# Softmax sums as four column tiles of 32, and a rounded copy moved from VectorE to ScalarE, in an attention and mixture-of-experts kernel

## The chip, the core and the metric

One core of a Trainium2 chip. The metric is the device time of one execution in microseconds, lower is better. The engines named below are TensorE (PE), VectorE (DVE), ScalarE (ACT), GpSimd (POOL) and SyncE (SP), which issues most of the transfers. PEld is TensorE's loading of weights.

## The reference

`x` and `ctx` are (4, 512, 512) in fp32: 4 batches of 512 rows (tokens) by 512. The first half is a cross-attention whose heads cut the row axis, so that 64 rows are one head and the 512 columns are positions; the softmax runs over 512 columns of `ctx`, after both sides are normalized over the 64 rows of a head:

```
qn, kn = l2norm over the head's 64 rows
qk = 5.0 * einsum('bhdq,bhdk->bhqk', qn, kn);  sm = softmax(qk)
x  = x + einsum('bhqk,bhdk->bhdq', sm, vh)        # q from layernorm(x), k = v = ctx
```

The second half is a mixture of 4 experts with top-2 routing and a capacity of 512 tokens each: router logits of 2048 tokens, a selection of the 512 best tokens per expert, then `gelu(tok @ W1[i]) @ W2[i] * p` with W1 512x2048 and W2 2048x512, added to the rows that were chosen.

## The kernel before, in words

The attention runs in 16 units of 128 rows, that is two heads each (`UNITS`, `unit(u, behind, ahead)`). Each engine has its own program for a unit, and the programs are written out by hand: what an engine does in unit n belongs partly to units n+1 to n+3 (statistics, normalized queries, keys) and partly to n-1 to n-3 (inverse sums, residual, router logits). `run_units` (lines 341 to 356) writes out units 0 to 3, runs units 4 to 11 as a loop of four rounds with two units in each, and writes out units 12 to 15. The arguments `behind` and `ahead` say how many units lie before and after, up to 4 and 3.

What the attention computes for a unit: TensorE transposes the normalized `x_norm` (`transpose_queries`, `bank_m`), ScalarE squares, VectorE sums (`sum_query_squares`), POOL takes the inverse root (`query_norms`), VectorE widens it (`widen_queries`, `wide_q`), TensorE transposes it back (`spread_queries`, `bank_m`), and VectorE multiplies: `queries(u, follow)` writes `q_f` (fp32), `q_hi` (rounded to fp32r) and `q_lo = q_f - q_hi`, with `normalize(follow)` of a later unit between them. Keys are split likewise into `k_hi` (ScalarE, `round_keys`) and `k_lo` (POOL). `scores(u, t)` on TensorE makes block t of four, 128 keys by 512 positions for both heads, out of three products. ScalarE's `exponentials(u, t)` takes them to `prob` (two instructions, one for each head). TensorE's `weighted_values` multiplies with the values, and `sums` adds the probabilities over the keys: VectorE has added the four blocks of `prob` in pairs (`half_sum[h][n]`, head h, half n), and `sums` multiplies them with a matrix of ones, 64 columns for each head, the two halves accumulated in PSUM (`o_ps[1]`).

ScalarE copies the result (`take_sums`, `p_sum`). Each row of a head's 64 is the same, so SyncE's `spread_inverse` takes one row per head, spreads it over 64 partitions as 8 numbers each (`few`, 128x8), VectorE inverts (`invert_few`), SyncE writes it to DRAM and reads it back broadcast (`p_inv`, 128x512), and `residual` multiplies one unit later. Only the last unit inverts the whole tile on VectorE (`invert_sums`).

The order of the work is set by each engine's own queue, which is strictly in order, and by semaphores. In the last third of a unit VectorE runs `residual`, `statistics_x2`, `widen_queries`, `take_logits` and `normalize_x2` of earlier and later units; `take_logits` (line 815) reads the router's result from `bank_t`, and TensorE's next unit begins with `values`, which writes `bank_t` (line 1246) and waits for it (line 1327). SyncE's order in the loop is, for each unit: load of a later x and ctx, `few`, `inv_dram`, `p_inv`, store of the sum and store of x2n (lines 443 to 451).

The experts follow: 16 chunks of `up` (line 1423) and `down` (lines 1450 to 1453) for each expert, with weights split into high and low parts.

Of the kernel before, what the change touches and what calls it, by code (L numbers as in the profile page):

```python
# [15 lines left out]
ALU = mybir.AluOpType  # L16
# [20 lines left out]
RAW_BUFS, SPLIT_BUFS = 2, 4  # L37
AHEAD = 2
FEW = 2 * D // P
DVE_HEADS, POOL_HEADS = (0, 1), ()  # L40
XT_AT = 10
FIND_AT = 8
# [51 lines left out]
def xattn_moe_kernel(nc, x, ctx_in, Wg, bg, W1, W2, consts, out):  # L94
# [6 lines left out]
    with ExitStack() as stack:  # L101
# [68 lines left out]
        with ExitStack() as phase:  # L170
# [16 lines left out]
            o_sb = [att(f"o_sb{n}", [P, D]) for n in range(2)]  # L187
            p_sum = att("p_sum", [P, D])
            half_sum = [[att(f"half_sum{h}{n}", [P, D]) for n in range(2)] for h in range(2)]
            few = att("few", [P, FEW])  # L190
            few_inv = att("few_inv", [P, FEW])
            p_inv = [att(f"p_inv{n}", [P, D]) for n in range(2)]
            o_norm = att("o_norm", [P, D])
# [76 lines left out]
        sums_ready = sem("sums_ready")  # L270
        sum_taken = sem("sum_taken")
        few_in = sem("few_in")
        few_done = sem("few_done")
        few_out = sem("few_out")
        inv_in = sem("inv_in")
# [93 lines left out]
        def _(sp):  # L369
# [34 lines left out]
            def spread_inverse(u):  # L404

                n = number(u)
                sp.wait_ge(sum_taken, n + 1)
                for h in range(2):
                    half = slice(h * P // 2, (h + 1) * P // 2)
                    sp.dma_start(few[half, :], p_sum[DH * h:DH * h + 1, :]).then_inc(few_in, 16)  # L410
                sp.wait_ge(few_done, n + 1)
                sp.dma_start(inv_dram.rearrange("(p j) -> p j", j=FEW), few_inv[:, :]).then_inc(few_out, 16)
                sp.wait_ge(few_out, 16 * (n + 1))
                for h in range(2):
                    sp.dma_start(p_inv[u[1]][DH * h:DH * (h + 1), :],
                                 inv_dram[D * h:D * (h + 1)].rearrange("(a d) -> a d", a=1).broadcast_to([DH, D])
                                 ).then_inc(inv_in, 16)
# [193 lines left out]
        def _(act):  # L611
# [25 lines left out]
            def round_keys(u, reused):  # L637
# [4 lines left out]
                    act.wait_ge(scores_ready, TT * (n - 1))  # L642
                nc.scalar.activation(k_hi[u[1]][:, :], c_sb[u[1]][:, :], ACT.Copy).then_inc(khi_done, 1)

            def exponentials(u, t, reused):
                g = TT * number(u) + t
                act.wait_ge(scores_ready, g + 1)
                if reused:
                    act.wait_ge(pv_done, g - TT + 1)
                    for h in range(2):  # L650
                        act.wait_ge(halves_done[h], 2 * (number(u) - 1) + t // 2 + 1)
                for h in range(2):
                    last = nc.scalar.activation(prob[h][t][:, :], s_ps[:, 2 * (t % 2) + h, :], ACT.Exp,  # L653
                                                scale=rnorm[u[1]][:, 0, t, h:h + 1])
                last.then_inc(exp_done, 1)
# [11 lines left out]
            def take_sums(u, reused):  # L667

                n = number(u)
                act.wait_ge(sums_ready, n + 1)  # L670
                if reused:
                    act.wait_ge(few_in, 32 * n)
                nc.scalar.activation(p_sum[:, :], o_ps[1][:, :], ACT.Copy).then_inc(sum_taken, 1)

            def take_x2t(u, bank=bank_t):
# [16 lines left out]
            take_v((0, 0), 0)  # L692
            square_queries((0, 1), True, o_ps[0])
            round_keys((0, 1), False)
            act.wait_ge(rk_done, 1)
            exponentials((0, 0), 0, False)
            exponentials((0, 0), 1, False)

            def unit(u, behind, ahead):
                if behind:  # L700
                    take_sums(before(u), behind > 1)
                if ahead:
                    square_keys(after(u), behind + 1)
                    take_v(after(u), behind + 1)
                exponentials(u, 2, behind > 0)
                exponentials(u, 3, behind > 0)
                if ahead > 1:
                    square_queries(after(after(u)), True)
# [62 lines left out]
        def _(dve):  # L771
# [46 lines left out]
            def queries(u, follow):  # L818


                n = number(u)
                dve.wait_ge(rq_ready, n + 1)
                nc.vector.scalar_tensor_tensor(q_f[:, :], x_norm[u[1]][:, :], ALPHA, bank_m[:, :], ALU.mult, ALU.mult
                                               ).then_inc(q_done, 1)
                nc.vector.scalar_tensor_tensor(q_hi[u[1]][:, :], x_norm[u[1]][:, :], ALPHA, bank_m[:, :],
                                               ALU.mult, ALU.mult).then_inc(qhi_done, 1)
                dve.wait_ge(q_done, n + 1)
                dve.wait_ge(qhi_done, n + 1)
                if follow is not None:
                    normalize(follow)  # L830
                nc.vector.tensor_tensor(q_lo[u[1]][:, :], q_f[:, :], q_hi[u[1]][:, :].bitcast(F32), ALU.subtract
                                        ).then_inc(q_split, 1)

# [6 lines left out]
            def invert_few(u):  # L840

                n = number(u)
                dve.wait_ge(few_in, 32 * (n + 1))
                nc.vector.reciprocal(few_inv[:, :], few[:, :]).then_inc(few_done, 1)

            def invert_sums(u):

# [386 lines left out]
        def _(pe):  # L1234
# [46 lines left out]
            def sums(u, behind, ahead):  # L1281
# [4 lines left out]
                    pe.wait_ge(sum_taken, number(u))  # L1286
                for n in range(2):
                    for h in range(2):
                        last = nc.tensor.matmul(o_ps[1][DH * h:DH * (h + 1), :], cst[:, C_ONES:C_ONES + DH],  # L1289
                                                half_sum[h][n][:, :], start=(n == 0), stop=(n == 1))  # L1290
                last.then_inc(sums_ready, 1)

            def transpose_x2(u, bank=bank_t):
# [26 lines left out]
            def unit(u, behind, ahead):  # L1320
# [14 lines left out]
                weighted_values(u, 0, behind > 0)  # L1335
                weighted_values(u, 1)
                if ahead > 1:
                    pe.wait_ge(qhi_done, n + 2)
                    transpose_queries(after(after(u)))
                if behind > 2:  # L1340
                    if ahead:
# [163 lines left out]
```

## Time and profile before

| | us |
|---|---|
| median of 3 runs (lowest, highest) | 624.82 (622.26, 625.44) |
| the profiled execution, its span | 624.58, 622.8 |
| busy: TensorE, VectorE, ScalarE, POOL | 568.2, 354.3, 281.6, 187.0 |
| attention, up to the last `sums` | about 200 |
| experts, from the first `up` | about 370 |

The span is the time from the first to the last instruction that the profiler saw; the profiled execution's own time contains 1.8 us around it. Busy times overlap, since the engines run side by side. The ends of matmuls are modelled. A time in brackets behind a row of the timeline is how long the engine was idle before it, and what ended that idle time.

### The profile page before, as it was taken

The page shows a single profiled execution, that of the slowest core. Times are in us where ns is not written, and L with a number is a line of the kernel's source. Part 1 is how long each engine was busy: PE and PEld are TensorE (multiplying, and loading weights), DVE is VectorE, ACT ScalarE, POOL GpSimd, SP SyncE. Part 2 cuts the span into 40 slices and gives each one's busy share as a digit, 9 for nine tenths or more (in the row PEclk, how much of TensorE's full clock was granted, in tenths as well). Part 3 has the DMA queues.
Part 4 walks back from the last instruction along what each step waited for, and adds up shares of the span by engine and source line. Part 5 has one row for each costly group of instructions (what it writes and reads, how often), then busy time and mean ns, then how long its engine had stood idle before and what let it go on. Part 6 is the DMA issues. An engine that isn't in the chain of part 4 may idle for free.

```text
span 622.8 us, 8726 instructions
## 1 busy us (share of the span) xinstructions
PE 568.2 (91%) x2842; PEld 408.5 (66%) x2842; DVE 354.3 (57%) x702; ACT 281.6 (45%) x421; POOL 187.0 (30%) x143
## 2 busy tenths in 40 slices
PE   3999999999998512999999999999999999999994
PEld 2545554554554401788888888888888788888883
DVE  5789998999888684443345443444633354423212
ACT  3777767767777130443333433334334324333220
POOL 8456566566551243100120330300510400500002
PEclk9999999999999655799999999999999999999998
DMA  4523423323213133323332543324451432542001
GB/s 146 196 60 119 137 86 118 126 94 109 96 53 118 52 115 96 95 100 128 97 113 88 183 149 120 118 84 134 152 184 69 137 124 76 190 149 68 0 1 67
DMA packets 46600, 67.73 MB, mean 109 GB/s; under 512 B 8560, under 2 KB 25072, under 8 KB 46576
## 3 DMA queue, kind: packets, MB, share of 16 engines
q1 hardware_dynamic: 42736, 54.84, 26.4%
q0 software_dynamic: 3840, 12.59, 6.2%
q8 instruction: 13, 0.21, 0.1%
q14 instruction: 11, 0.09, 0.0%
HBM read 54.70 MB, written 12.64 MB: 108 GB/s over the span
## 4 chain that ended last, share of the span: by engine, by line
PE 65%; DVE 5%; issue 4%; DMA 1%; POOL 1%; POOLq 0%; DVEq 0%; ACT 0%; SPq 0%
PE two L1423 29%; PE four L1453 9%; PE four L1452 9%; PE four L1450 9%; PE two L1277 2%; PE four L1267 2%; DVE junk L1046 1%; PE two L1289 1%; PE bank_t L1305 1%; DMA x_got<-x2n_dram,idx_all 1%; POOL w_lo L533 1%; DMA p_inv<-inv_dram 0%; PE bank_t L1411 0%; PE bank_m L1411 0%; DVE onehot L1133 0%
## 5 line engine op out<-in xcount | busy, mean ns | idle before, releaser
L759 ACT ACTIVATE h_f<-two 128x512 f32<-128x512 f32 x64 | 38.3, 599 | 231.2 <-PE two L1423 231.2
L1207 DVE TENSOR_TENSOR h_lo<-h_f,h_hi 128x512 fp32r<-128x512 f32 x64 | 44.1, 689 | 125.7 <-ACT h_hi L760 125.7
L1423 PE MATMUL two<-xt_hi,w_hi 128*128 (+1 forms) x256 | 102.9, 402 | 0.7 <-ACT xt_hi L748 0.7
L1423 PE MATMUL two<-xt_hi,w_lo 128*128 (+1 forms) x256 | 101.3, 396 | 0.0
L1453 PE MATMUL four<-w_hi,h_lo 128*128 128x512 f32 x256 | 100.5, 393 | 0.0
L1423 PE MATMUL two<-xt_lo,w_hi 128*128 (+1 forms) x256 | 100.5, 395 | 0.0
L1450 PE MATMUL four<-w_hi,h_hi 128*128 128x512 f32 x256 | 100.5, 392 | 0.0
L1452 PE MATMUL four<-w_lo,h_hi 128*128 128x512 f32 x256 | 100.4, 392 | 0.0
L653 ACT ACTIVATE prob<-four,rnorm 128x512 f32<-128x512 f32 x128 | 77.6, 688 | 28.6 <-POOL rnorm L476 17.6
L1177 DVE TENSOR_TENSOR w_lo<-raw,w_hi 128x2048 fp32r<-128x2048 f32 x30 | 68.7, 2290 | 23.3 <-ACT w_hi L686 23.3
L476 POOL TENSOR_TENSOR rnorm<-ss_max,power 128x8 f32<-128x8 f32 x32 | 64.7, 2024 | 51.5 <-DVE ss_max L808 45.3
L606 POOL DMA_INDIRECT out<-o_got,idx_all x16 | 20.2, 1264 | 165.4 <-DVE o_got L1228 163.0
L585 POOL DMA_INDIRECT x_got<-x2n_dram,idx_all x16 | 23.9, 1496 | 139.9 <-DVE idx_all L1164 125.1
L1277 PE MATMUL two<-prob,v_t 128*64 128x512 f32 x256 | 62.0, 605 | 0.0
L686 ACT ACTIVATE w_hi<-raw 128x2048 fp32r<-128x2048 f32 x32 | 61.3, 1918 | 0.0
L1423 PEld LDWEIGHTS two<-xt_hi,w_hi 128*128 128x128 f32 x256 | 48.6, 190 | 11.7 <-ACT xt_hi L748 1.1
L1423 PEld LDWEIGHTS two<-xt_hi,w_lo 128*128 128x128 f32 x256 | 48.6, 190 | 11.1
L1423 PEld LDWEIGHTS two<-xt_lo,w_hi 128*128 128x128 f32 x256 | 48.5, 189 | 10.7
L1450 PEld LDWEIGHTS four<-w_hi,h_hi 128*128 128x128 f32 x256 | 48.1, 188 | 10.9
L1453 PEld LDWEIGHTS four<-w_hi,h_lo 128*128 128x128 f32 x256 | 48.1, 188 | 10.8
L1452 PEld LDWEIGHTS four<-w_lo,h_hi 128*128 128x128 f32 x256 | 48.1, 188 | 10.6
L856 DVE TENSOR_TENSOR half_sum<-prob 128x512 f32<-128x512 f32 x64 | 41.5, 689 | 0.1
(177 smaller groups left out, 741.5 us busy)
## 6 DMA issues: line engine op xcount, KB each, us to landing
raw<-in_L_ffn_W SPq DMA_DIRECT2D x64, 512.0 KB, 4.0
x_all<-in_x SPq DMA_DIRECT2D x16, 256.0 KB, 2.9
c_sb<-in_ctx SPq DMA_DIRECT2D x16, 256.0 KB, 2.8
out<-x_all SPq DMA_DIRECT2D x16, 256.0 KB, 2.0
x2n_dram<-x2n SPq DMA_DIRECT2D x16, 256.0 KB, 2.0
p_inv<-inv_dram SPq DMA_DIRECT2D x30, 128.0 KB, 2.8
few<-p_sum SPq DMA_DIRECT2D x30, 2.0 KB, 2.2
cst<-in_consts SPq DMA_DIRECT2D x1, 354.5 KB, 5.0
```

The source lines that it names most:

```text
L476: return nc.gpsimd.tensor_tensor(dst, src, power[:, 0:n], ALU.pow)
L653: last = nc.scalar.activation(prob[h][t][:, :], s_ps[:, 2 * (t % 2) + h, :], ACT.Exp, scale=rnorm[u[1]][:, 0, t, h:h + 1])
L686: nc.scalar.activation(w_hi[c % SPLIT_BUFS][:, :], raw[c % RAW_BUFS][:, :], ACT.Copy).then_inc(whi_done, 1)
L759: nc.scalar.activation(h_f[m % 2][:, :], z_ps[m % 2][:, :], ACT.Gelu)
L856: nc.vector.tensor_tensor(half_sum[h][n][:, :], prob[h][2 * n][:, :], prob[h][2 * n + 1][:, :], ALU.add).then_inc(halves_done[h], 1)
L1177: nc.vector.tensor_tensor(w_lo[c % SPLIT_BUFS][:, :], raw[c % RAW_BUFS][:, :], w_hi[c % SPLIT_BUFS][:, :].bitcast(F32), ALU.subtract).then ...
L1207: nc.vector.tensor_tensor(h_lo[m % 2][:, :], h_f[m % 2][:, :], h_hi[m % 2][:, :].bitcast(F32), ALU.subtract).then_inc(h_split, 1)
L1277: last = nc.tensor.matmul(o_ps[0][DH * h:DH * (h + 1), :], v_t[u[1]][:, t, h, :], prob[h][t][:, :], start=(t == 0), stop=(t == TT - 1))
L1423: return nc.tensor.matmul(z[:, :], w_part[c][:, w], x_k, start=start, stop=stop)
L1450: nc.tensor.matmul(acc_ps[:, t, :], h_hi[m % 2][:, h], w_hi[c][:, w], start=(m == 0), stop=False)
L1452: nc.tensor.matmul(acc_ps[:, t, :], h_hi[m % 2][:, h], w_lo[c][:, w], start=False, stop=False)
L1453: last = nc.tensor.matmul(acc_ps[:, t, :], h_lo[m % 2][:, h], w_hi[c][:, w], start=False, stop=(m == MT - 1))
```

## The change

Three edits, which are independent of each other:

- `sums`: in all units but the last, the four products (two heads, two halves) each go to a tile of 32 columns of their own, to partitions 0, 32, 64 and 96 of the same bank, without accumulation. `QUAD` is 32.
- The halves are now added later: SyncE carries four rows instead of two, into a `few` of 128x16 (the two halves side by side), and VectorE adds them (`few_sum`) before the reciprocal, which waits for that addition.
- `q_hi` is no longer computed by VectorE from PSUM; ScalarE copies it from `q_f` (`round_queries`), between the exponentials of block 2 and block 3. VectorE runs `normalize(follow)` directly behind `q_f`, then waits for q_hi, then `q_lo`. TensorE's next transposes into `bank_m` wait for `q_f` only.

```diff
+QUAD = P // 4
-            few = att("few", [P, FEW])
+            few = att("few", [P, 2 * FEW])
+            few_sum = att("few_sum", [P, FEW])
...
-                    sp.dma_start(few[half, :], p_sum[DH * h:DH * h + 1, :]).then_inc(few_in, 16)
+                    for m in range(2):
+                        row = QUAD * (2 * m + h)
+                        sp.dma_start(few[half, m * FEW:(m + 1) * FEW], p_sum[row:row + 1, :]).then_inc(few_in, 16)
...
+            def round_queries(u):
+
+                act.wait_ge(q_done, number(u) + 1)
+                nc.scalar.activation(q_hi[u[1]][:, :], q_f[:, :], ACT.Copy).then_inc(qhi_done, 1)
...
                 exponentials(u, 2, behind > 0)
+                if ahead:
+                    round_queries(after(u))
                 exponentials(u, 3, behind > 0)
...
-                nc.vector.scalar_tensor_tensor(q_hi[u[1]][:, :], x_norm[u[1]][:, :], ALPHA, bank_m[:, :],
-                                               ALU.mult, ALU.mult).then_inc(qhi_done, 1)
+                if follow is not None:
+                    normalize(follow)
                 dve.wait_ge(q_done, n + 1)
                 dve.wait_ge(qhi_done, n + 1)
-                if follow is not None:
-                    normalize(follow)
...
-                dve.wait_ge(few_in, 32 * (n + 1))
-                nc.vector.reciprocal(few_inv[:, :], few[:, :]).then_inc(few_done, 1)
+                dve.wait_ge(few_in, 64 * (n + 1))
+                nc.vector.tensor_tensor(few_sum[:, :], few[:, 0:FEW], few[:, FEW:2 * FEW], ALU.add
+                                        ).then_inc(few_added, 1)
+                dve.wait_ge(few_added, n + 1)
+                nc.vector.reciprocal(few_inv[:, :], few_sum[:, :]).then_inc(few_done, 1)
...
-                        last = nc.tensor.matmul(o_ps[1][DH * h:DH * (h + 1), :], cst[:, C_ONES:C_ONES + DH],
-                                                half_sum[h][n][:, :], start=(n == 0), stop=(n == 1))
+                        if ahead:
+
+                            row = QUAD * (2 * n + h)
+                            last = nc.tensor.matmul(o_ps[1][row:row + QUAD, :], cst[:, C_ONES:C_ONES + QUAD],
+                                                    half_sum[h][n][:, :], start=True, stop=True,
+                                                    tile_position=(0, row))
...
-                    pe.wait_ge(qhi_done, n + 2)
+                    pe.wait_ge(q_done, n + 2)
```

VectorE's queue in the first unit of the loop, from the statistics to the second key sum, before. `ISA` and `REGISTER_ALU` rows carry waits and loop counters; line numbers are those of each kernel.

```order
L782 TENSOR_SCALAR var_e<-mv 128x1
L822 ISA
L823 SCALAR_TENSOR_TENSOR q_f<-x_norm,bank_m 128x512
L825 SCALAR_TENSOR_TENSOR q_hi<-x_norm,bank_m 128x512
L788 ISA
L788 TENSOR_SCALAR x_norm<-x_all,mv,rstd 128x512
L831 TENSOR_TENSOR q_lo<-q_f,q_hi 128x512
L805 TENSOR_REDUCE ss<-c_sq 128x8
```

The same stretch of VectorE after the change:

```order
L795 TENSOR_SCALAR var_e<-mv 128x1
L835 ISA
L836 SCALAR_TENSOR_TENSOR q_f<-x_norm,bank_m 128x512
L801 ISA
L801 TENSOR_SCALAR x_norm<-x_all,mv,rstd 128x512
L842 TENSOR_TENSOR q_lo<-q_f,q_hi 128x512
L818 TENSOR_REDUCE ss<-c_sq 128x8
```

One large instruction is gone, and `q_lo` waits for another engine where it waited for its own.

ScalarE's queue in the second unit of the loop, from the copy of the values to the squares, before:

```order
L633 ACTIVATE v_t<-bank_t 128x512
L647 REGISTER_ALU
L649 REGISTER_ALU
L651 REGISTER_ALU
L653 ACTIVATE prob<-four,rnorm 128x512 x2
L647 REGISTER_ALU
L653 ACTIVATE prob<-four,rnorm 128x512 x2
L615 REGISTER_ALU
L618 ACTIVATE x_sq<-bank_m 128x512
```

The same stretch of ScalarE after the change:

```order
L638 ACTIVATE v_t<-bank_t 128x512
L657 REGISTER_ALU
L659 REGISTER_ALU
L661 REGISTER_ALU
L663 ACTIVATE prob<-four,rnorm 128x512 x2
L653 ACTIVATE q_hi<-q_f 128x512
L657 REGISTER_ALU
L663 ACTIVATE prob<-four,rnorm 128x512 x2
L620 REGISTER_ALU
L623 ACTIVATE x_sq<-bank_m 128x512
```

q_hi stands behind two exponentials of block 2 and ahead of two of block 3.

## Rows read from the trace of the kernel before

**Rows 1.** Windows by unit: length, then busy us (instructions) of each engine

```profile
core 0: us, PE busy (x) PEld busy (x) DVE busy (x) ACT busy (x) POOL busy (x), PEclk, DMA share, GB/s
108.49:120.50 12.01, 11.74 (x73) 6.33 (x73) 10.88 (x27) 8.77 (x16) 7.18 (x6) 1.00 0.34 110
```

**Rows 2.** Waits of TensorE from 60 to 180 us

```profile
engine line waited for: us in total, times, longest us
PE bank_t L1246 <- DVE logits L815: 1.0, 4, 0.3
```

**Rows 3.** Timeline of units 1 and 2: start, length, engine, line, operation, idle before

```profile
30.73 2.42 ACT L653 ACTIVATE prob<-four,rnorm 128x512 f32<-128x512 f32 x4 [0.26 <-PE four L1267]
...
31.66 0.68 DVE L831 TENSOR_TENSOR q_lo<-q_f,q_hi 128x512 fp32r<-128x512 f32 x1
...
35.27 2.42 ACT L653 ACTIVATE prob<-four,rnorm 128x512 f32<-128x512 f32 x4 [0.80 <-POOL rnorm L476]
...
39.06 0.60 ACT L673 ACTIVATE p_sum<-two 128x512 f32<-128x512 f32 x1 [0.35 <-PE two L1289]
...
40.97 2.42 ACT L653 ACTIVATE prob<-four,rnorm 128x512 f32<-128x512 f32 x4 [0.25 <-PE four L1267]
```

**Rows 4.** Timeline of the first unit of one round of the loop

```profile
96.46 0.15 DVE L815 TENSOR_TENSOR logits<-bank_t,bgb 128x4 f32 x1
...
96.74 0.65 PE L1246 MATMUL bank_t<-cst,c_sb 128*128 128x128 f32 x4 [0.31 <-DVE logits L815]
...
98.99 2.42 ACT L653 ACTIVATE prob<-four,rnorm 128x512 f32<-128x512 f32 x4 [0.47 <-PE four L1267]
...
100.39 0.69 DVE L831 TENSOR_TENSOR q_lo<-q_f,q_hi 128x512 fp32r<-128x512 f32 x1
...
106.59 1.89 PE L1289 MATMUL two<-half_sum,cst 128*64 128x512 f32 x8
...
106.72 0.65 ACT L643 ACTIVATE k_hi<-c_sb 128x512 fp32r<-128x512 f32 x1
```

**Rows 5.** Timeline of the unit behind it

```profile
108.20 0.15 DVE L815 TENSOR_TENSOR logits<-bank_t,bgb 128x4 f32 x1
...
110.46 0.69 DVE L823 SCALAR_TENSOR_TENSOR q_f<-x_norm,bank_m 128x512 f32<-128x512 f32 x1
...
110.75 2.42 ACT L653 ACTIVATE prob<-four,rnorm 128x512 f32<-128x512 f32 x4 [0.41 <-PE four L1267]
...
111.07 0.68 DVE L825 SCALAR_TENSOR_TENSOR q_hi<-x_norm,bank_m 128x512 fp32r<-128x512 f32 x1
...
111.52 1.14 SPq L410 DMA_DIRECT2D few<-p_sum  x2
...
111.96 0.55 DVE L788 TENSOR_SCALAR x_norm<-x_all,mv,rstd 128x512 f32 x1 [0.21 <-issue]
...
112.42 0.68 DVE L831 TENSOR_TENSOR q_lo<-q_f,q_hi 128x512 fp32r<-128x512 f32 x1
...
115.14 0.19 DVE L844 RECIPROCAL few_inv<-few 128x8 f32<-128x8 f32 x1
...
120.21 0.16 DVE L815 TENSOR_TENSOR logits<-bank_t,bgb 128x4 f32 x1
```

**Rows 6.** Transfers into `few`, 96 to 156 us

```profile
DMA to landing us min/median/max: 2.0/2.3/2.5
```

**Rows 7.** Timeline of the units behind the loop

```profile
155.68 0.15 DVE L815 TENSOR_TENSOR logits<-bank_t,bgb 128x4 f32 x1
...
157.91 2.42 ACT L653 ACTIVATE prob<-four,rnorm 128x512 f32<-128x512 f32 x4 [0.24 <-PE four L1267]
...
159.52 0.68 DVE L831 TENSOR_TENSOR q_lo<-q_f,q_hi 128x512 fp32r<-128x512 f32 x1
...
167.00 0.15 DVE L815 TENSOR_TENSOR logits<-bank_t,bgb 128x4 f32<-128x4 f32 x1
...
178.17 0.15 DVE L815 TENSOR_TENSOR logits<-bank_t,bgb 128x4 f32<-128x4 f32 x1
...
181.72 0.69 DVE L831 TENSOR_TENSOR q_lo<-q_f,q_hi 128x512 fp32r<-128x512 f32 x1
...
190.29 0.69 DVE L868 TENSOR_TENSOR o_norm<-o_sb,p_inv 128x512 f32<-128x512 f32 x1 [0.91 <-DMA p_inv<-inv_dram]
```

More of the change, by code:

```diff
@@ L272, in xattn_moe_kernel @@
         few_in = sem("few_in")
+        few_added = sem("few_added")
         few_done = sem("few_done")
@@ L671, in take_sums @@
                 if reused:
-                    act.wait_ge(few_in, 32 * n)
+                    act.wait_ge(few_in, 64 * n)
                 nc.scalar.activation(p_sum[:, :], o_ps[1][:, :], ACT.Copy).then_inc(sum_taken, 1)
@@ L694, in _ @@
             round_keys((0, 1), False)
+            round_queries((0, 0))
             act.wait_ge(rk_done, 1)
@@ L1288, in sums @@
                     for h in range(2):
-                        last = nc.tensor.matmul(o_ps[1][DH * h:DH * (h + 1), :], cst[:, C_ONES:C_ONES + DH],
-                                                half_sum[h][n][:, :], start=(n == 0), stop=(n == 1))
+                        if ahead:
[3 more added lines that the diff above has]
+                                                    tile_position=(0, row))
+                        else:
+                            last = nc.tensor.matmul(o_ps[1][DH * h:DH * (h + 1), :], cst[:, C_ONES:C_ONES + DH],
+                                                    half_sum[h][n][:, :], start=(n == 0), stop=(n == 1))
                 last.then_inc(sums_ready, 1)
```

## The prediction

> **What bounds the kernel now.** I read the windows by attention unit first, then the waits, then the timeline of all engines over two units of the loop. One unit of the loop shows TensorE busy 11.74 of 12.01 us, VectorE 10.88, ScalarE only 8.77 [rows 1]. So TensorE looks like the bound. The waits say that it is not quite: in ten units TensorE idles only 1.0 us in all, and always for VectorE's `logits` [rows 2], which frees `bank_t` for the next transposes. In the timeline, one unit after the other, `logits` starts at 96.46, 108.20 and 120.21, so a pair of units takes 23.75 us. TensorE begins its unit at 96.74, after an idle of 0.31 that `logits` ended [rows 4, 5]. VectorE's own row of work is as long as TensorE's. Two engines are bounds at nearly the same time: TensorE before and after the loop, VectorE and TensorE together inside it. A change has to help both, and the chain that ties them has to stay short.
>
> That chain, which I call the ring, runs so: VectorE `logits` (unit n-1), then TensorE transposes and scores for unit n, then ScalarE's exponentials of score block 2. So far it went no further, since VectorE made q_hi itself. After the change ScalarE makes q_hi between blocks 2 and 3, and VectorE's `q_lo` waits for it. VectorE is strictly in order, so everything behind `q_lo` waits too, down to the next `logits`. The ring closes.
>
> **The sums.** The four matmuls of `sums` take 1.89 us as two pairs that run side by side on 64 columns each [rows 4]. With four tiles of 32 columns side by side they would take half, about 0.95, so TensorE gains 0.9 us a unit in 15 units. This is worth something only where TensorE is what ends last. The Trainium skill ("TensorEngine Tiling (Array Packing)", Tiling Modes) lists 128x32 as four tiles that work independently, and says that a change of mode drains the array; the rows here show only the 64-column form, so neither half is tested yet.
>
> **VectorE loses 0.6 us and gets a wait.** q_hi is 0.68 us long and took 0.61 of the queue; the idle of 0.21 ahead of `x_norm` goes as well [rows 5]. When could `q_lo` start? The exponentials of block 2 start 98.99 - 96.46 = 2.53 and 110.75 - 108.20 = 2.55 us after `logits` [rows 4, 5]; they wait for TensorE, which waits for `logits`, so this distance stays. Four exponentials take 2.42 with a last one of 0.69, so two take 1.15. Then q_hi: the same kind of copy, SBUF to SBUF with rounding, takes 0.65 for the keys [rows 4]. I allow 0.04 for the handover. So `q_lo` starts 2.54 + 1.15 + 0.65 + 0.04 = 4.38 after `logits`. Before it started 100.39 - 96.46 = 3.93 and 112.42 - 108.20 = 4.22 after it. q_f is done at 111.15 while ScalarE is free at 110.75 + 1.15 = 111.90, so the exponentials hold q_hi up, not q_f. The time that VectorE is given turns into idle in front of `q_lo`, and `q_lo` is even later than before by 0.45 and 0.16.
>
> **From q_lo to the next logits** nothing gets shorter: 108.20 - 100.39 = 7.81 and 120.21 - 112.42 = 7.79 [rows 4, 5], queued back to back. Added is the sum of the two halves, a 128x8 operation in front of the dependent reciprocal, whose own 0.19 us [rows 5] I take as its price; say 0.2. One unit: 4.38 + 7.80 + 0.20 = 12.38, a pair 24.76 against 23.75.
>
> **The transfers to `few`.** SyncE issues two in 1.14 us, 0.57 each, from 111.52 [rows 5]. Four put the last issue at 111.52 + 1.71 = 113.23. It lands 2.0, 2.3 or 2.5 us later [rows 6]: 115.23, 115.5 or 115.7. VectorE wants it at 108.20 + 4.38 + (115.14 - 112.42) = 115.30. So 0 to 0.4 us of wait, and I take 0.2 in one unit of each pair (in the other the issues stand a little earlier). SyncE starts these issues after the store of x2n, so if VectorE is late they are late too; the wait isn't absorbed. Behind them on SyncE stand only the stores of the inverse sums, which are needed a whole unit later inside the loop. Bounds for this term: none at all, and 0.4 in every unit (12 units, 4.8 us).
>
> The loop has 8 units: (24.76 + 0.2 - 23.75) x 4 = **+4.8 us**.
>
> **Units before the loop.** Here TensorE is the bound: from 30.73 to 40.97 is 10.24 us [rows 3]. ScalarE takes over. q_lo would start 1.15 + 0.65 + 0.04 = 1.84 after the exponentials, was 31.66 - 30.73 = 0.93. From q_lo over the key norms to the next exponentials is 35.27 - 31.66 = 3.61, and ScalarE waits for POOL's rnorm there (0.80) [rows 3]. From those to the next block 2 is 40.97 - 35.27 = 5.70, of which 0.35 and 0.25 are idle and can close: 5.10. Sum 1.84 + 3.61 + 5.10 = 10.55, 0.3 more than now. Two or three units of this; some of the 3.61 was itself waiting, so I take **+0.4**. Bounds: -2.7, if all three units win the full 0.9 of the sums, and +2.7, if q_lo's 0.9 stands each time.
>
> **Units after the loop.** Exponentials 157.91 - 155.68 = 2.23 after `logits`, so q_lo at 2.23 + 1.84 = 4.07; then 167.00 - 159.52 = 7.48 and 0.2: 11.75, with half of the 0.2 for the transfers 11.85. Two units 23.7; now 178.17 - 155.68 = 22.49 [rows 7]. **+1.2**. In the unit after, q_lo goes from 181.72 - 178.17 = 3.55 to 4.07: **+0.5**. Its reciprocal starts the chain store, load, `o_norm` at 190.29, which VectorE waits for (0.91, DMA) [rows 7], so it is passed on whole. Two more of the 0.2 additions stand on that last chain: **+0.4**. The last unit keeps the old sums.
>
> Behind that the search for the thresholds and the experts follow, with the same instructions as now. Nothing there gets longer or shorter.
>
> **Sum.** 0.4 + 4.8 + 1.2 + 0.5 + 0.4 = +7.3 us. The profiled execution took 624.58 us (span 622.8), which gives 631.9; the median of the three runs is 0.24 higher, 632.1. I say **632.1 us**, 1.2% slower.
>
> **Rivals.**
> 1. *Later transfers.* As the forecast, but the last of four transfers lands 2.5 us or more after its issue, and VectorE waits in all 12 units. Against the 0.8 us that I counted for it in the loop and 0.2 behind it, 0.4 x 12 = 4.8 gives +3.8: 636. For it: 2.5 is in the rows [rows 6]. Against: the median of 2.3.
> 2. *The other side: q_hi comes in time.* If q_hi were finished early, VectorE's row would shorten: 11.87 (half of 23.75) - 0.61 - 0.21 + 0.2 = 11.25, plus 0.3 since q_f (0.68), the copy (0.65) and the handover leave VectorE at least that much idle behind `x_norm`. 11.55 against 11.87 in 8 units is -2.6, 0.9 in each of three early units -2.7, and 0.3 in the three late ones: 624.8 - 6.2 = 618.6. It decides at one point: q_hi must be ready before 3.9 us after `logits`, so ScalarE must be free at 3.2. It is free at 3.69, because block 2 of the scores ends when it does. Only if TensorE could get ahead of `logits` would this change; the wait of 0.31 there [rows 4] is against it.
> 3. *Four column tiles don't run side by side.* Then `sums` is four matmuls of 0.95 each, 3.8 us, and TensorE's unit 11.74 + 1.9 = 13.6; 15 units of which TensorE is the bound: 1.8 x 15 = +27, 652. The pairs that do overlap in the rows speak against it, and so does the skill's page named above.
> 4. *The clock.* TensorE will now idle 12.4 - 10.85 = 1.5 us a unit. Every window in the loop is at a granted clock of 1.00 [rows 1]. If it fell to half for even one unit, TensorE's 10.85 us would become up to 21.7, 9 more than the 12.4 of the ring: up to 641. The Trainium skill ("TensorE: Matmul & The Clock Gate", HAM oscillation) warns of idle gaps between bursts of matmuls; no row of this loop has such a gap, so it is untested.
> 5. *Nothing.* The early and late units win what the loop loses: 625 to 627. It needs the early bound of -2.7 and no wait for `few`.
>
> **Chances.** Forecast 0.68, later transfers 0.12, in time 0.07, column tiles 0.03, clock 0.03, nothing 0.07. The forecast's own range, with the early term from -2.7 and the transfers from none to half of their bound, is 628.5 to 635. For 8 in 10 I widen to the later transfers: 628 to 636.5. What this measurement can tell from no change is about 0.5%, 3.1 us: 621.7 to 627.9. Slower 0.87, within it 0.06, faster 0.07.
>
> **What would show it.** Right: an idle of 0.9 to 1.1 us in front of `q_lo`, ended by ScalarE's q_hi, in every unit of the loop; q_hi starting at once behind the second exponential; `logits` to `logits` 12.3 to 12.6 us; the group of `sums` on 32 columns at about 0.95 us for four and an idle of about 1.5 us in front of TensorE's `bank_t` transposes, ended by `logits`; VectorE's busy time down about 8 us (16 x 0.68 less, 15 x 0.19 more) and ScalarE's up about 10 (16 x 0.65), with a longer span. Wrong: `q_lo` right behind `x_norm`; transposes that follow the sums without a gap; a span at or below 622.8; or a loop unit under 12.2 us. If `few_sum` shows an idle of over 0.3 us ended by the DMA in each unit, rival 1 holds.

## The result, and the profile after

The changed kernel takes **632.61 us** (median of 4 runs, 632.27 to 634.89), the kernel before 623.81 beside it. The ratio is **1.015**, with a 95% interval of 1.0122 to 1.0178. The profiled execution has a span of 630.5 us, before 622.8. The kernel before had 624.82 as its median in the three runs of the table above and has 623.81 in the four beside the changed kernel, so the medians differ by 8.8 us; the spans differ by 7.7.

First the windows of two units of the loop, from one start of TensorE's work on `bank_t` to the next. The columns are those of [rows 1]: length, then busy time and instructions of each engine, granted clock, DMA share, GB/s.

```profile
86.58:99.00 12.42, 11.01 (x72) 5.92 (x73) 10.46 (x27) 9.01 (x16) 7.16 (x6) 1.00 0.35 110
99.00:111.43 12.43, 11.02 (x73) 5.91 (x73) 10.32 (x27) 9.02 (x16) 7.12 (x6) 1.00 0.31 104
```

TensorE is busy 0.7 us less than in the unit of [rows 1], and the unit is 0.4 longer (0.57 by the mean of eight, see the table below): now neither TensorE nor VectorE fills it. The clock stays at 1.00, the upper of its two levels (2.4 GHz), though TensorE idles 1.4 us a unit.

What ends the idle time, from 60 to 185 us (engine, line, waited for: total, times, longest):

```profile
PE bank_t L1260 <- DVE logits L828: 14.1, 10, 1.6
...
DVE q_lo L842 <- ACT q_hi L653: 11.3, 10, 1.4
...
DVE few_sum L855 <- DMA few<-p_sum: 0.8, 1, 0.8
```

The 1.0 us of [rows 2] has become 14.1, and the engine that is waited for, VectorE, itself waits 11.3 us for ScalarE. The timeline of one unit shows why (start, length, engine, line, operation, idle before):

```profile
98.71 0.15 DVE L828 TENSOR_TENSOR logits<-bank_t,bgb 128x4 f32 x1
...
99.00 0.65 PE L1260 MATMUL bank_t<-cst,c_sb 128*128 128x128 f32 x4 [1.41 <-DVE logits L828]
...
100.81 0.68 DVE L836 SCALAR_TENSOR_TENSOR q_f<-x_norm,bank_m 128x512 f32<-128x512 f32 x1
...
101.23 1.26 ACT L663 ACTIVATE prob<-four,rnorm 128x512 f32<-128x512 f32 x2 [0.45 <-PE four L1281]
...
102.39 0.63 ACT L653 ACTIVATE q_hi<-q_f 128x512 fp32r<-128x512 f32 x1
...
103.11 0.69 DVE L842 TENSOR_TENSOR q_lo<-q_f,q_hi 128x512 fp32r<-128x512 f32 x1 [1.16 <-ACT q_hi L653]
...
105.86 0.16 DVE L855 TENSOR_TENSOR few_sum<-few 128x8 f32<-128x8 f32 x1
106.05 0.20 DVE L858 RECIPROCAL few_inv<-few_sum 128x8 f32<-128x8 f32 x1
...
108.95 1.07 PE L1306 MATMUL two<-half_sum,cst 128*32 128x512 f32 x8
...
111.14 0.15 DVE L828 TENSOR_TENSOR logits<-bank_t,bgb 128x4 f32 x1
```

q_f was ready at 101.49, but q_hi begins at 102.39, right behind block 2's exponentials; `q_lo` follows at 103.11, 4.40 us behind `logits`. Before it was 3.93 and 4.22 [rows 4, 5]. The sums did become shorter, 1.07 us against 1.89 [rows 4], and the gain is lost in the 1.41 in front of the next transposes.

The chain of waits, in order of time (start, length, what), goes once around:

```profile
101.23 0.34 ACT prob L663
...
102.39 0.64 ACT q_hi L653
...
103.11 0.69 DVE q_lo L842
...
111.14 0.17 DVE logits L828
...
111.43 0.65 PE bank_t L1260 x4
...
112.52 0.91 PE four L1281 x6
...
113.67 0.49 ACT prob L663
```

Over the whole attention `q_lo` waited 20.2 us (groups by line: busy, mean ns, then idle before it):

```profile
L842 DVE TENSOR_TENSOR q_lo<-q_f,q_hi 128x512 fp32r<-128x512 f32 x16 | 11.1, 693 | 20.2 <-ACT q_hi L653 20.2
```

### The profile page after: what moved, and what is told of

Its sections match the earlier page's. It is cut to its first block, busy times and chain, and to the rows that moved or that the text cites. A ratio compares the mean times of both kernels' runs of the same rounds, so it can differ in the third digit from the quotient of the medians.

```text
span 630.5 us, 8771 instructions
## 1 busy us (share of the span) xinstructions
PE 559.2 (89%) x2842; PEld 403.2 (64%) x2842; DVE 347.4 (55%) x701; ACT 287.7 (46%) x437; POOL 186.8 (30%) x143
## 4 chain that ended last, share of the span: by engine, by line
PE 62%; DVE 15%; issue 9%; ACT 5%; POOL 4%; DMA 2%; SPq 1%; DVEq 0%; ACTq 0%; POOLq 0%
PE two L1444 29%; PE four L1474 9%; PE four L1473 9%; PE four L1471 9%; DVE half_sum L870 2%; ACT prob L663 2%; PE four L1281 2%; POOL rnorm L481 2%; DVE q_lo L842 2%; ACT q_hi L653 1%; DVE ss L818 1%; DVE x_all L884 1%; DVE ss L808 1%; DVE o_norm L882 1%; PE bank_t L1260 1%
## 5 line engine op out<-in xcount | busy, mean ns | idle before, releaser
L663 ACT ACTIVATE prob<-four,rnorm 128x512 f32<-128x512 f32 x128 | 79.4, 692 | 34.7 <-POOL rnorm L481 26.8
L611 POOL DMA_INDIRECT out<-o_got,idx_all x16 | 20.2, 1264 | 165.5 <-DVE o_got L1242 163.0
```

## The experiments

Two theories were compared. *The ring*: `logits`, TensorE, exponentials, q_hi, `q_lo`, next `logits`. *The transfers*: four issues to `few` instead of two. Each kernel was run beside the kernel before, whose median was 623.7 to 624.6; where two kernels were run beside different runs of it, their ratios compare better than their medians. "Loop unit" is the distance of two `logits` in the timeline, mean over the eight units of the loop. A name with `few_` in front has the issues to `few` earlier on SyncE, one with `fill` or `all_moves` also another order on VectorE; each is described where its result is read.

| kernel | us | ratio to before (95%) | loop unit | `q_lo` waits for q_hi, each unit of the loop | `few_sum` waits for the DMA |
|---|---|---|---|---|---|
| before | 623.7 | 1 | 11.85 | – | none |
| changed | 632.6 | 1.0122 to 1.0178 | 12.42 | 1.0 to 1.2 | 0.26 and 0.75, outside the loop |
| `sums_only` | 626.7 | 1.0036 to 1.0063 | 12.18 | – | 0.31, 1.16, 0.46 |
| `qhi_only` | 629.9 | 1.0087 to 1.0117 | 12.32 | 1.0 to 1.5 | 0.32 once (reciprocal) |
| `between` | 628.7 | 1.0057 to 1.0086 | 12.20 | 0.4 to 0.7 | 0.4 in five of eight, 1.60 behind the loop |
| `both_early` | 630.1 | 1.0085 to 1.0119 | 12.50 (12.29 without the first) | 0.3 to 0.6 | 0.3 to 0.5, 2.31 in the first |
| `few_after` | 631.6 | 1.0098 to 1.0127 | 12.42 | 1.0 to 1.3 | none |
| `few_sums` | 624.4 | 0.9996 to 1.0016 | 12.07 | – | 0.67 once, behind the loop |
| `few_between` | 622.8 | 0.9977 to 1.0000 | 11.85 | 0.4 to 0.7 | none |
| `few_fill_sums` | 620.2 | 0.9931 to 0.9963 | 11.64 | – | none |
| `few_fill_between` | 619.7 | 0.9914 to 0.9946 | 11.52 | none | none |
| `all_moves_before` | 624.1 | 0.9983 to 1.0003 | 11.67 | – | none |
| `all_moves_between` | 620.0 | 0.9915 to 0.9940 | 11.57 | 0.77 | none |
| `all_moves_sums` | 618.7 | 0.9908 to 0.9933 | 11.43 | – | none |

### Each part by itself

`sums_only` keeps the column tiles, the four transfers and the addition, and undoes the rest:

```diff
-                exponentials(u, 2, behind > 0)
-                if ahead:
-                    round_queries(after(u))
+                exponentials(u, 2, behind > 0)
...
+                nc.vector.scalar_tensor_tensor(q_hi[u[1]][:, :], x_norm[u[1]][:, :], ALPHA, bank_m[:, :], ...
```

> The changed kernel with q_hi back on VectorE; the four column tiles, the four transfers and the added halves stay. Theory (the ring over q_hi is what cost the time, the sums only add 0.2 us of VectorE work a unit): no idle in front of q_lo; loop unit 11.85 + 0.2 = 12.05, +1.5 us over 8 units; the three early units, which TensorE bounds, win up to 0.85 each, -2.3; behind the loop 0 to +0.3. In all -0.6 against before: 623.2. Rival 1 (the sums' longer way over four transfers and an addition is what cost it): 628 or more, with a DMA wait in front of few_sum. Rival 2 (TensorE is the bound everywhere): 15 x 0.8 less, 612.

`qhi_only` is the kernel before with the other part:

```diff
                 exponentials(u, 2, behind > 0)
+                if ahead:
+                    round_queries(after(u))
...
-                nc.vector.scalar_tensor_tensor(q_hi[u[1]][:, :], x_norm[u[1]][:, :], ALPHA, bank_m[:, :],
-                                               ALU.mult, ALU.mult).then_inc(qhi_done, 1)
+                if follow is not None:
+                    normalize(follow)
```

> The kernel before with only the move of q_hi to ScalarE; sums, transfers and reciprocal as before. Theory (ring): q_lo 4.4 us behind logits, idle about 1.1 in front of it; loop unit 12.43 - 0.19 = 12.24, +3.1 us over 8 units; early units, where the sums lie on the same ring (half sums late, then sums), about 0.8 longer than with the short sums, +3; behind the loop +0.5. In all +6.5: 630.3. Rival (the transfers or the addition cost it): within 1 us of before, 624.

q_hi alone costs 6.3 us, as expected (6.5). The parts of that sum were off and made up for each other: by the `logits` of the traces the units ahead of the loop cost 0.8 us where 3 were expected, the loop 3.7 for 3.1, and what follows 1.8 for 0.5. The sums alone were expected to gain 0.6 and cost 3.0. Their part on TensorE works (1.07 us), and the early units win 2.1 us as expected; what was missed is a wait of VectorE for the transfers, at its largest behind the loop:

```profile
163.97 0.17 DVE L854 TENSOR_TENSOR few_sum<-few 128x8 f32<-128x8 f32 x1 [1.16 <-DMA few<-p_sum]
```

### Shortening the detour of q_hi

`between` puts q_hi between the two heads' exponentials of block 2 (`then` is the unit after u):

```diff
                 for h in range(2):
+                    if h == 1 and then is not None:
+                        round_queries(then)
                     last = nc.scalar.activation(prob[h][t][:, :]
```

> The changed kernel with q_hi between the two exponentials (head 0, head 1) of block 2 instead of behind both. Theory (ring): q_f is done 2.95 us behind logits and the first exponential 3.12, so q_hi starts 0.58 earlier, q_lo at 3.83 instead of 4.41; loop unit 12.43 - 0.58 = 11.85, -4.6; early and late units -0.5 each in five or six, -2.7. In all 632.6 - 7.3 = 625.3. Rival (ScalarE's load as such, 0.63 more a unit, is what costs, wherever it stands): no difference, 632.6.

`both_early` leaves q_hi and moves VectorE's `logits` ahead of `residual`, and `widen_queries` ahead of `statistics_x2`, so that TensorE may start earlier.

```diff
+                if behind > 2:
+                    take_logits(before(before(before(u))))
                 if behind > 1 and ahead:
                     residual(before(before(u)))
+                if ahead > 1:
+                    widen_queries(after(after(u)))
                 if behind > 1 and ahead:
                     statistics_x2(before(before(u)))
-                if ahead > 1:
-                    widen_queries(after(after(u)))
-                if behind > 2:
-                    take_logits(before(before(before(u))))
```

> The changed kernel with VectorE's take_logits moved ahead of the residual and widen_queries moved ahead of statistics_x2, so that TensorE may begin the next unit about 2 us earlier; q_hi as in the changed kernel. Theory (ring): the ring through TensorE and ScalarE goes slack, the 1.0 to 1.1 us of idle in front of q_lo shrinks to about 0.3 (q_f, copy, handover against x_norm), TensorE's idle in front of bank_t shrinks or moves; x2n then waits 0.5 us longer for POOL, since the two moved instructions filled that wait. Loop unit about 11.9; in all 632.6 - 5.5 = 627. Rival (VectorE waits for ScalarE's load, not for the position of logits): idle in front of q_lo stays at 1.0, and with the longer x2n wait the kernel gets slower, 635 to 637.

Both moved the right way, and brought about half or less of what was expected: 3.9 and 2.5 us. In both the idle time of `q_lo` fell as it should (0.43 in the middle of `between`, 0.31 in most units of `both_early`), but VectorE then waited at `few_sum`. In `both_early` this takes back all that the loop had to win: its eight units take 100.0 us against 99.4 in the changed kernel, 2.31 of them one wait at `few_sum` in the first, and the 2.5 us are won behind the loop. The row here is from `between`:

```profile
116.12 0.17 DVE L855 TENSOR_TENSOR few_sum<-few 128x8 f32<-128x8 f32 x1 [0.39 <-DMA few<-p_sum]
```

This suggests a second ring, just below the first: x2n, its store on SyncE, the two loads, the four issues, their landing, `few_sum`, and VectorE's row to the next x2n. In the changed kernel the first ring would hide it. SyncE's row there:

```profile
111.67 0.55 DVE L906 TENSOR_SCALAR x2n<-x_all,mv,rstd 128x512 f32 x1 [0.38 <-POOL rstd L481]
...
112.25 0.34 SPq L405 DMA_DIRECT2D x2n_dram<-x2n  x1
...
113.35 0.35 SPq L375 DMA_DIRECT2D x_all<-in_x  x1
...
114.05 0.34 SPq L380 DMA_DIRECT2D c_sb<-in_ctx  x1
...
114.55 2.42 SPq L415 DMA_DIRECT2D few<-p_sum  x4
```

`p_sum` was complete at 111.06, and the issues begin 3.5 us later. In `between` no landing in the loop took longer than 2.4 us, so its waits come from late issues and not from slow transfers.

### Breaking the second ring

`few_sums`, `few_between` and `few_after` are `sums_only`, `between` and the changed kernel, with one edit on SyncE: the issues of a unit stand ahead of the store of x2n, where the order was store of x2n, loads, issues. What the store and what the loads cost was not told apart.

```diff
                 spread_rest((h - 2, 1))
-                store_unit((h - 2, 0))
+                store_x2((h - 2, 0))
+                issue_few((h - 1, 0))
+                store_x2n((h - 2, 0))
                 load_next_x((h + 1, 1))
                 load_next_c((h + 1, 0))
```

> The sums change alone (q_hi on VectorE), with one change on SyncE: the four issues to few stand ahead of the store of x2n and of the two loads, instead of behind them. Theory (a second ring just below the first: x2n, its store, two loads, four issues of 0.6 us, landing, few_sum, and so on to the next x2n): the waits of few_sum for the DMA (0.31, 1.16 and 0.46 in the run of the sums change alone) vanish, the issues begin about 2 us earlier, and the time falls by their sum and some 0.3: 624.5, against 626.66. Loop unit 12.05 to 12.18, since VectorE's row is full there. Rival (the waits come from the landing or from the late sums themselves, not from what stands ahead on SyncE): waits stay, 626.5.

> All of the change, with q_hi between the two heads' exponentials of block 2, and the four issues to few ahead of the store of x2n and the loads on SyncE. Theory of the second ring: without it the waits of few_sum (0.4 in every other unit, 1.60 in unit 12) go; loop unit from 12.2 to about 11.95, less 1.2 in unit 12: 625.5, against 628.74. Rival (the loop unit was set by the idle of q_lo and by VectorE's row, and the waits only shift): loop unit stays at 12.2, only unit 12 gains: 627.5.

> The changed kernel, with only the four issues to few ahead of the store of x2n and of the loads on SyncE. Theory (two rings: the one through ScalarE's q_hi is the slower, 12.42 us, and hides the one through the transfers): loop unit stays at 12.42, q_lo still waits 1.0 to 1.2 us, only the 0.75 that few_sum waited in unit 12 and some of the next is won: 631.5, against 632.6. Rival (the place of the transfers is the main cost of the change, as their place was worth 6.0 us where q_hi came between the heads): 627 to 628.

The theory held for `few_sums` (624.4) and for `few_after` (631.6): in the changed kernel the loop unit doesn't move at all, 12.42, since the first ring sets it, and the same edit is worth 6.0 us where that ring is shorter. The gain of `few_after` is small and not measured well: 1.0 us by the medians, 2.4 by the ratios, whose intervals overlap, and 0.8 by the spans. `few_between` did better than expected (622.8 against 625.5). There the issues come early:

```profile
106.11 0.60 ACT L701 ACTIVATE p_sum<-two 128x512 f32<-128x512 f32 x1 [0.16 <-PE two L1322]
...
106.50 0.15 DVE L844 TENSOR_TENSOR logits<-bank_t,bgb 128x4 f32 x1
...
106.73 2.40 SPq L417 DMA_DIRECT2D few<-p_sum  x4
...
110.34 0.69 DVE L858 TENSOR_TENSOR q_lo<-q_f,q_hi 128x512 fp32r<-128x512 f32 x1 [0.43 <-ACT q_hi L669]
```

The prediction's arithmetic fits here too: `q_lo` 110.34 - 106.50 = 3.84 behind `logits`, then 8.00 to the next one at 118.34, makes 11.84, the unit that is measured. In the changed kernel it is 103.11 - 98.71 = 4.40 and 111.14 - 103.11 = 8.03.

### Is the change worth anything in a kernel whose order suits it?

Three moves in VectorE's row were added: the two of `both_early`, and the first statistics of a later unit into the wait of x2n for POOL ("fill", the statistics of the unit three ahead). POOL makes rstd of x2n first.

```diff
-                if ahead > 2:
+                if ahead > 2 and behind < 2:
                     statistics(after(after(after(u))))
...
+                if ahead > 2 and behind > 1:
+                    statistics(after(after(after(u))))
                 if behind > 1 and ahead:
                     normalize_x2(before(before(u)), behind > 3)
```

> The sums change alone with the issues to few first on SyncE, and three moves in VectorE's row: logits ahead of the residual, the widening ahead of the second statistics, and the first statistics of three units ahead inside the wait of x2n for POOL's rstd. Theory (with q_hi on VectorE its row is the bound, 11.07 busy of 12.18, and the gaps are x2n's 0.4 and x_norm's 0.2): unit about 11.6, 8 x 0.5 less than the same kernel without the moves, some more before and behind the loop: 619. Then this is faster than the kernel before by 0.7%. Rival (the time is bound by the ring through TensorE, which starts its unit at logits, or by the issues): unit 12.0 or more, 623 to 625.

> All of the change with q_hi between the two heads' exponentials, the issues to few first on SyncE, and the same three moves in VectorE's row. Theory (with both rings short, VectorE busy 10.4 a unit and the gaps filled): loop unit 11.4, 619 or a little below, and q_hi on ScalarE then costs nothing or gains 0.2 a unit against the sums change alone. Rival (q_lo still waits for ScalarE, which waits for TensorE, so that what VectorE saves turns into idle again): unit 11.8 to 12, 623 to 625, slower than the same with q_hi on VectorE.

Both reach the direction and nearly the time (620.2 and 619.7 against 619), and both are faster than before. The unit is 11.64 for about 11.6 expected in the first, and 11.52 for 11.4 in the second. In the second `x_norm` lies beside POOL's `k_lo`:

```profile
108.03 1.27 POOL L521 TENSOR_TENSOR k_lo<-c_sb,k_hi 128x512 fp32r<-128x512 f32 x1
108.20 1.38 DVE L817 TENSOR_SCALAR x_norm<-x_all,mv,rstd 128x512 f32 x1
...
L817 DVE TENSOR_SCALAR x_norm<-x_all,mv,rstd 128x512 f32 x8 | 11.2, 1402 | 0.0
```

(The last line is the group by line, in the loop: 1402 ns on average, 546 in the kernel before.) So the moves were made in another form: x_norm of the unit three ahead, then the statistics of the unit four ahead, both in front of x2n. The three kernels of this form differ only in the parts of the change.

```diff
+                if ahead > 2 and behind > 1:
+                    normalize(after(after(after(u))))
+                    if not isinstance(u[0], int) or u[0] < UNITS // 2 - 2:
+                        statistics(after(after(after(after(u)))))
                 if behind > 1 and ahead:
                     normalize_x2(before(before(u)), behind > 3)
```

> The kernel before (sums as two pairs of 64 columns, q_hi on VectorE) with every move of order that the next kernel has: issues to few first on SyncE, logits ahead of the residual, widening ahead of the second statistics, and x_norm of three units ahead and the first statistics of four units ahead inside the wait of x2n for POOL. Theory (TensorE is a bound of its own here at 11.74 a unit, VectorE's row only beside it): loop unit 11.75 to 11.85 and TensorE idle near zero, 622.5. Rival (VectorE's row was the only bound): 619 or less.

> The whole change with q_hi between the two heads' exponentials and every move of order of the kernel above. In the run with the earlier form of the moves x_norm took 1.40 us instead of 0.54 each time that it stood beside POOL's k_lo; here it stands ahead of x2n, after which k_lo starts. Theory: x_norm takes 0.55 again, VectorE is busy about 10.3 a unit and TensorE 11.0, so TensorE is the bound: unit 11.1 to 11.3, 616, faster than before by 1.2% and by 1% than the kernel before with the same moves, which is what the two parts of the change are worth. Rival (another wait stands at 11.55, the four transfers or POOL's rnorm): unit 11.5, 619.5.

> The sums change alone, with q_hi on VectorE and all moves of order of the last two kernels. In the run with q_hi on ScalarE, q_lo waited 0.77 us for it in each unit and the unit stood at 11.57. Theory (the detour through ScalarE still is the ring: q_f, q_hi, q_lo, the key norms, POOL's rnorm, the exponentials): q_hi in VectorE's own row costs 0.61 instead of 0.77, and x_norm no longer stands behind it, so the unit falls to 11.3 to 11.45 and the time to 618.5. Rival (what holds the unit at 11.57 doesn't go through q_hi, but through TensorE, busy 11.0, and the transfers): 620.0 to 620.5, unit 11.55 to 11.6. Second rival (VectorE's row, busy 10.9, becomes the bound again): 621 or more.

Windows of one unit of the loop, with the columns of [rows 1], of `all_moves_before`:

```profile
115.40:127.05 11.65, 11.65 (x74) 6.33 (x72) 10.90 (x28) 8.35 (x15) 6.63 (x6) 1.00 0.32 113
```

The same of `all_moves_between`:

```profile
103.24:114.69 11.45, 11.43 (x76) 5.82 (x72) 10.27 (x29) 8.93 (x17) 7.35 (x6) 1.00 0.34 116
```

And of `all_moves_sums`:

```profile
101.70:113.10 11.40, 11.22 (x74) 5.88 (x72) 10.88 (x31) 8.42 (x17) 7.35 (x6) 1.00 0.34 116
```

- Without the change TensorE is busy in all of its unit, 93.33 of 93.33 us in the loop, and these moves win nothing (0.9993, interval across 1). Other orders of the kernel before were not run.
- With the column tiles the same moves give 0.9921: 0.7% less than `all_moves_before`, intervals apart. Here the 0.8 us that TensorE is given arrives in part. This has the lowest median of all, 5 us under the kernel before and 14 under the changed one; the intervals of `all_moves_between` and `few_fill_between` overlap with its own.
- `all_moves_between` missed: x_norm is back at 543 ns as expected, but the time is 620.0 instead of 616, and the unit 11.57. So the long x_norm was not what held the unit at 11.52 in `few_fill_between`, or another wait took its place. q_hi now waits for q_f, and q_lo for q_hi:

```profile
108.81 0.63 ACT L669 ACTIVATE q_hi<-q_f 128x512 fp32r<-128x512 f32 x1 [1.09 <-DVE q_f L852]
...
109.55 0.69 DVE L858 TENSOR_TENSOR q_lo<-q_f,q_hi 128x512 fp32r<-128x512 f32 x1 [0.77 <-ACT q_hi L669]
```

The detour through ScalarE takes 109.55 - 108.09 = 1.46 us from q_f to `q_lo`; in `all_moves_sums`, where VectorE makes q_hi, it is 119.37 - 117.98 = 1.39. The ratios differ by 0.06% and their intervals overlap. The medians (620.0 and 618.7) and the loop (8 x 0.14 us) put q_hi on ScalarE about 1.2 us behind, but the kernel before was also 0.9 us slower beside the first, so these runs do not tell which is better.
- The theory for `all_moves_sums` held (618.7, unit 11.43, against 618.5 and 11.3 to 11.45). Why `all_moves_between` stands at 11.57, with TensorE busy 11.4 of it, is not settled: no run took q_hi's detour away there without giving VectorE its work back. Nor is 11.4 TensorE's bound: the same matmuls are busy for 11.0 us a unit in `few_between`.

## Why the prediction was right

The forecast was 632.1, measured are 632.6. The nearness is partly luck: the forecast was +7.3 us, and the medians differ by 8.8, but the kernel before came out 1.0 us lower than the runs that the forecast started from; and within the sum, terms that were too small and too large offset each other. The range of 628.5 to 635 doesn't follow from its own terms: the early bound of -2.7 and no transfers give 632.1 - 3.1 - 1.0 = 628.0, and half of the transfers' bound gives 633.5. Step by step, by the traces:

- *q_lo behind logits.* Predicted 4.38, measured 4.40 and, one unit later, 115.56 - 111.14 = 4.42. The wait is ended by q_hi in every unit of the loop, as said.
- *From q_lo to the next logits.* 7.80 + 0.20, measured 8.03. The added operation moves the reciprocal by 106.05 - 105.86 = 0.19.
- *Transfers in the loop.* Mis-sized: 0.2 in each pair, measured none. The transfers land 1.8 / 2.0 / 2.3 us (least, median, greatest) behind their issue, against 2.0 / 2.3 / 2.5 in [rows 6], and the last of four, for which the prediction took 2.3, lands after 1.8 in each of the eight units; the long ones are the first of each four. This made the loop +4.58 instead of +4.8: `logits` at 61.46 and 160.83, before at 60.89 and 155.68 [rows 7].
- *Entering the loop.* +0.4 predicted, +0.57 measured. The 0.8 us of the sums in each early unit were lost: `q_lo` waited 1.7 to 2.1 us for q_hi, and the sums themselves waited for `half_sum` (0.8 and 0.7). The bound of -2.7 was not approached; `sums_only` without q_hi did have shorter units there, 9.51 against 10.24.
- *Two units behind the loop.* Too small: +1.2 predicted, +1.98 measured (173.49 and 185.30 against 167.00 and 178.17). The missing part is one wait, 0.75:

```profile
168.40 0.17 DVE L855 TENSOR_TENSOR few_sum<-few 128x8 f32<-128x8 f32 x1 [0.75 <-DMA few<-p_sum]
```

  The last of these four took 2.9 us to land. This is rival 1 at one place of twelve. `few_after` has no such wait, and its two units behind the loop take 23.62 us, against 24.47.
- *The last two terms.* +0.5 was +0.79 (`logits` at 196.00, before 188.08), and +0.4 was -0.44 (`o_norm` at 206.64, before 199.16), where a write of the inverse sums to DRAM landed sooner, 1.4 us (issued at 192.47) where it had been 2.1 (184.56). That is not an effect that the forecast had, and no run shows that the change brings it. Together +0.35 for +0.9. At that point the kernel is 7.48 us late, for a predicted 7.3: the parts of the sum missed by +0.17, -0.22, +0.78 and -0.55.

The rivals:

- *Later transfers* (636): not in the loop of the changed kernel. As the prediction states it, by landings of 2.5 us or more, it held once, with 2.9. The waits that appeared as soon as the first ring was shortened (`between`) have another cause, issues that start late on SyncE; they are 2.2 of the 3.0 us that `sums_only` costs (626.7 against 624.4).
- *q_hi in time* (618.6): refuted by the idle of 1.16. The prediction said what would bring it about, TensorE getting ahead of `logits`. `few_fill_between`, which does so among other moves, came to 619.7; there `q_lo` has no idle time in the loop, but stands behind an x_norm of 1.4 us, which covers it.
- *Four column tiles that don't run side by side* (652): refuted. The group of `sums` (eight records for the four products, in both kernels) lasts 1.07, where two tiles of 64 took 1.89. The independence that the Trainium skill's page "TensorEngine Tiling (Array Packing)" (Tiling Modes) states is what the trace shows. The group takes 0.12 more than the 0.95 of the forecast; whether that is the drain that the prediction took from there, no row tells.
- *The clock* (641): refuted. 1.00 in every window of the loop with 1.4 us of idle a unit.
- *Nothing* (625 to 627): the early units won nothing.
- *Busy times.* VectorE's fell by 6.9 (8 said), ScalarE's rose by 6.1 (10 said), though q_hi's own group is the 10.2 us expected, 16 x 636 ns. No group of ScalarE became shorter: added up they rise from 299.5 to 312.2. An engine's busy time counts a stretch in which two of its records overlap only once, and q_hi begins at 102.39, before the end of the exponentials at 102.49. The forecast added up records where it should have added what each takes of the queue; for VectorE, 16 x 0.61 less and 15 x 0.19 more gives the 6.9.

The chain was read rightly, but it is not the whole cause. By the medians of the runs, q_hi alone costs 6.3 us, the sums alone 3.0, both together 8.8. That looks additive, but stage by stage it isn't: entering the loop the two parts cost +0.8 and -2.1 alone and +0.6 together, since q_hi's ring takes what the sums win; in the loop +3.7 and +2.7 alone and +4.6 together, since the longer ring hides the other. The forecast put nearly all of it on one ring; the second it named only as a price per unit, and did not see that it is a ring of its own.

## What to carry to other kernels

Work that is moved from a full engine to a free one has a price if its result comes back later than before: count from the event that starts both, here `logits`, and include what is queued ahead on the engine that takes it over. With `q_lo` 4.40 us behind `logits` the move cost time; with 3.84, against 3.93 and 4.21 in `few_sums`, `few_between` is 1.7 us under `few_sums`. When one ring is shortened, look up which queue stands next: here four issues on SyncE, whose place was worth 1 to 2 us under the longer ring and 6 us under the shorter. And a part that wins nothing can be worth something after a change of order: the column tiles cost 0.5% by themselves, nothing that can be measured with the transfers issued earlier (the kernel before with that edit alone was not run), and are the difference of 0.7% in the best order found.

## What the hardware showed beside this

- *VectorE beside POOL.* A `TENSOR_SCALAR` of 128x512 (`x_norm`) took 1402 ns in the loop in `few_fill_between`, where it began 0.1 to 0.2 us behind the start of POOL's `TENSOR_TENSOR` (`k_lo`), and 543 to 546 in the loops of the kernel before and of `all_moves_between`, where it lay apart from it. It ended 0.28 us behind POOL's end (109.58 against 109.30), and POOL's own 1.27 did not change. Twice in `few_fill_sums` it began 0.9 us behind the start of `k_lo`, took 660 ns, and again ended about 0.3 behind POOL. What this costs the kernel is not shown: without it, in another order, the unit was 11.57 where it had been 11.52. The Trainium skill, "SBUF — State Buffer" (Who interferes with whom), says that a `tensor_scalar` can take the pair of ports that VectorE shares with GpSimd, and that whoever issues first holds it for a whole instruction. The rows fit that; which mode the instruction runs in is not in them. The operations with one source in PSUM that lay beside `k_lo` in `all_moves_sums`, q_f and q_hi, kept their 0.68.
- *Issuing.* Each small issue on SyncE takes 0.6 us (median 596 ns of 20), four of them 2.4. The last of four landed 1.8 us behind its issue, the last of two 2.0 to 2.4, so in the loop four transfers cost by the 1.2 us more that they hold the queue, and not by their landing.
- *Handover.* From the end of ScalarE's q_hi (102.39 + 0.63 = 103.02) to VectorE's `q_lo` (103.11) is 0.09 us; 0.04 had been allowed.
